# A six-layer graph network on one core: the first layer's second stretch with its gathered rows split into two f32r terms

## The reference

```python
xn = layernorm(x)
h = xn                                   # graph network, 6 layers
for layer in range(6):
    agg = segment_sum(h[src], dst)       # gather a row per edge, add it to its node
    z = relu(batchnorm((h + agg) @ W1[layer] + b1[layer]))
    z = batchnorm(z @ W2[layer] + b2[layer])
    h = z if layer == 5 else relu(z)
# mixing, 8 heads of 32 columns: k, v = layernorm of xn per head (two weight sets)
mix = q @ (k^T v / N) + xn
x = x + h + mix
y = layernorm(x)
x = x + sum_e softmax(y @ Wr + br)_e * expert_e(y)   # 8 experts, 3 matrices each
```

## Time and profile before

| What | Value |
|---|---|
| median of the runs | 4614.98 us (4611.78 to 4618.43) |
| profiled execution | 4616.16 us, its span 4614.4 us |
| mean granted TensorE clock | 0.981 |
| busy, of the span | PE 95%, PEld 70%, DVE 66%, ACT 68%, POOL 65% |
| fp32 matmuls of gathered quads (L975) | 1072, from 84.8 to 817.9 us |
| f32r matmuls of gathered quads (L978) | 1750, from 969.4 us on |

### The profile page before, as it was taken

How to read it: one execution, slowest core, us unless ns; L and a number is a source line. 1 busy time by engine, 2 the same in 40 slices (tenths; PEclk the granted TensorE clock), 3 DMA queues, 4 the chain that set the end, 5 groups by cost and what they waited for, 6 DMA issues and landing times.

```text
span 4614.4 us, 69574 instructions
## 1 busy us (share of the span) xinstructions
PE 4399.7 (95%) x18931; PEld 3237.0 (70%) x18931; DVE 3056.1 (66%) x7493; ACT 3122.7 (68%) x4292; POOL 2987.3 (65%) x3420
## 2 busy tenths in 40 slices
PE   4999899999999999999998999999998899999999
PEld 3666688578866888578875888668875766666665
DVE  6888766466665666656765666656665466666666
ACT  5767533488866888578876888578875555555555
POOL 5777766057771777447772777637773277778786
PEclk8999999999999999999999999999999799999999
DMA  6444644065543555255543555345554000000000
GB/s 228 159 136 154 214 155 145 17 201 177 172 137 123 179 177 172 80 178 181 171 146 115 176 180 162 115 142 187 172 157 170 10 3 6 8 9 8 9 8 9
DMA packets 198882, 571.18 MB, mean 124 GB/s; under 512 B 44498, under 2 KB 63420, under 8 KB 198396
## 3 DMA queue, kind: packets, MB, share of 16 engines
q0 software_dynamic: 109728, 299.78, 22.3%
q1 hardware_dynamic: 81404, 238.40, 14.8%
q10 hardware_dynamic: 7392, 28.90, 1.6%
HBM read 487.16 MB, written 79.74 MB: 123 GB/s over the span
## 4 chain that ended last, share of the span: by engine, by line
PE 75%; issue 6%; POOL 5%; DVE 5%; ACT 4%; DMA 3%; ACTq 0%; DVEq 0%; POOLq 0%; SPq 0%
PE bank L1077 33%; PE bank L1287 12%; PE bank L1296 7%; PE bank L978 6%; PE bank L1172 5%; PE bank L975 4%; POOL BIG L799 4%; PE bank L1021 3%; DMA BIG<-y_table,idx 2%; PE bank L1106 1%; ACT Z L1339 1%; ACT bank L1374 1%; PE bank L986 1%; DVE BIG L1628 1%; DMA G<-y_table,idx 1%
## 5 line engine op out<-in xcount | busy, mean ns | idle before, releaser
L799 POOL DMA_INDIRECT BIG<-y_table,idx x1750 | 1665.7, 952 | 575.4 <-issue 521.5
L1077 PE MATMUL bank<-Ac,Ych 128*128 128x512 f32 x6204 | 1474.8, 391 | 0.0
L1077 PEld LDWEIGHTS bank<-Ac,Ych 128*128 128x128 f32 x6204 | 1164.4, 188 | 244.4 <-issue 1.0
L1393 ACT CAST Ac<-BIG 128x2048 fp32r<-128x2048 uint8 (+1 forms) x426 | 738.7, 1748 | 183.7 <-PE bank L978 89.5
L1644 DVE TENSOR_TENSOR Gsp<-bank,Gsp 128x512 fp32r<-128x512 f32 x870 | 559.7, 683 | 226.6 <-ACT bank L1374 225.7
L1768 DVE TENSOR_TENSOR Z<-Z,bank 128x512 f32 x546 | 375.2, 687 | 462.6 <-PE bank L978 270.7
L799 POOL DMA_INDIRECT G<-y_table,idx x536 | 536.8, 1001 | 199.1 <-issue 154.8
L2140 DVE TENSOR_TENSOR G<-G,bank 128x448 f32<-128x448 f32 x784 | 461.4, 618 | 218.5 <-ACT G L1565 112.8
L1367 ACT CAST Gsp<-BIG 128x1024 fp32r<-128x1024 f32 (+1 forms) x455 | 461.1, 1014 | 165.2 <-DMA BIG<-y_table,idx 150.6
L1374 ACT COPY bank<-BIG 128x512 f32<-128x512 f32 x870 | 481.0, 583 | 127.3 <-DVE Gsp L1644 127.2
L1654 DVE TENSOR_SCALAR onehot<-iota,rel 128x128 fp32r<-128x128 f32 x2290 | 517.1, 302 | 11.2 <-PE bank L975 6.6
(11 more groups left out here) (233 smaller groups left out, 6104.9 us busy)
## 6 DMA issues: line engine op xcount, KB each, us to landing
BIG<-adjacency SPq DMA_DIRECT2D x273, 448.0 KB, 3.6
BIG<-y_table,idx POOLq DMA_INDIRECT x1750
BIG<-y_table SPq DMA_DIRECT2D x27, 896.0 KB, 5.8
y_table<-BIG SPq DMA_DIRECT2D x25, 896.0 KB, 3.9
adjacency<-BIG ACTq DMA_DIRECT2D x7, 3136.0 KB, 12.5
BIG<-in_x SPq DMA_DIRECT2D x14, 896.0 KB, 8.4
G<-y_table,idx POOLq DMA_INDIRECT x536
y_table<-BIG ACTq DMA_DIRECT2D x7, 896.0 KB, 3.6
```

The lines of the kernel that those rows point to most:

```text
L799: nc.gpsimd.indirect_dma_start(out=rows[:, j, :], out_offset=None, in_=y_table, in_offset=bass.IndirectOffsetOnAxis(ap=idx[:, t:t + 1], ax ...
L1077: last = mm(bank[2 * (k % 2) + b][:, 0:UW], Ych[pos % 2][:, i, s, b * P:(b + 1) * P], cast_place(l, x_)[:, i - CA * h, :], start=(i == 0 a ...
L1393: nc.scalar.copy(cast_place(l, x_)[:, 0:t1 - t0, :], Land[k % NL][:, t0:t1, :]).then_inc(s_ac, 1)
```

## The change

In steps n >= N1 of the first layer a quad is handled as in the later layers:

- *Buffers.* Three buffers `Gsp0`: two in `G` (over the old `raw0`), the third in `BIG` at the place of the third `Ac`, so two `Ac` are left for the first layer's casts (`casts` returns 2). The raw rows land in the low half of the buffer itself (`raw_split`), on new semaphores `s_gx`. `place0` gives the buffer, quad 91 the second one, quad 92 the first, quad 93 the third.
- *Gather.* Quad n waits for quad n - 3. Quad 91 waits for quad 90 and quad 92 for quad 89, the last ones in their place. Quad 93 waits for the store of the last adjacency block; ScalarE's cast no longer does.
- *ScalarE.* `quad_high(n)` behind the casts of step n: one copy 128x1024, rounded. The square root `mixing` comes behind it and a step later (`set_at(n, 2)`).
- *VectorE.* `quad_low(n)` at the head of step n: one in-place subtraction 128x1024. Groups of the second stretch are evicted by the 128x512 reduction.
- *TensorE.* `quad(n)` goes behind the dense halves and the transposes of step n, ahead of the mixing product; one 512 wide f32r matmul per tile.

```diff
         def casts(l):
-            return NAC if first_layer(l) else NACL
+            return NAC - 1 if first_layer(l) else NACL
+        def place0(n):
+            return (N1 % RQ0 // 2, 1 - N1 % RQ0 // 2, 2)[(n - N1) % 3]
+        def last_there(n):
+            if n >= N1 + 3:
+                return n - 3
+            return max((m for m in range(N1) if m % RQ0 // 2 == place0(n)), default=None)
...
             def gather(l, n):
                 rows, s_rows, _ = gathered(l, n)
-                if first_layer(l):
+                if first_layer(l) and n >= N1:
+                    if last_there(n) is not None:
+                        hold(pool, s_mmq, last_there(n) + 1)
+                    else:
+                        hold(pool, s_fl[(S - 1) % 2], (S - 1) // 2 * LANES + LANES)
+                elif first_layer(l):
...
-                    if first_layer(l):
+                    if not is_split(l, n):
                         last = mm(group_bank(g)[:, 0:D], onehot[:, q, j, :].bitcast(fp32), rows[:, j, :],
                                   start=start, stop=stop)
                     else:
                         last = mm(group_bank(g)[:, 0:2 * D], onehot[:, q, j, :],
-                                  Gsp[n % RQ][:, j, :, :].rearrange("p k f -> p (k f)"), start=start, stop=stop)
+                                  split_place(l, n)[:, j, :, :].rearrange("p k f -> p (k f)"), start=start, stop=stop)
...
                 for n in range(quads(l)):
-                    if first_layer(l):
+                    if first_layer(l) and n < N1:
                         quad(l, n)
...
                     if first_layer(l):
+                        if n >= N1:
+                            quad(l, n)
                         if set_at(n, MIX_LAG) is not None:
...
                 act.wait_ge(s_rows, there)
+                if first_layer(l):
+                    nc.scalar.copy(split_place(l, n)[:, 0:tiles(n), 0, :], rows[:, 0:tiles(n), :]).then_inc(s_gh, 1)
+                    return
...
-                if first_layer(l) and x_ == NAC - 1:
-                    act.wait_ge(s_fl[(S - 1) % 2], (S - 1) // 2 * LANES + LANES)
...
                             half(x_)
-                        if set_at(n, 1) is not None:
-                            mixing(set_at(n, 1))
+                        quad_high(l, n)
+                        if set_at(n, 2) is not None:
+                            mixing(set_at(n, 2))
...
             def quad_low(l, n):
-                dve.wait_ge(s_gh, (l - 1) * N1 + n + 1)
+                dve.wait_ge(s_gh, split_before(l) + n + 1)
+                if first_layer(l):
+                    there = split_place(l, n)
+                    tt(there[:, 0:tiles(n), 1, :], gathered(l, n)[0][:, 0:tiles(n), :],
+                       there[:, 0:tiles(n), 0, :].bitcast(fp32), ALU.subtract).then_inc(s_gl, 1)
+                    return
...
-                if first_layer(l):
+                if first_layer(l) and g < NGR:
                     V.tensor_copy(grow[:, g % 2, :], group_bank(g)[:, 0:D]).then_inc(s_ev, 1)
                 else:
                     V.tensor_reduce(grow[:, g % 2, :], group_bank(g)[:, 0:2 * D].rearrange("p (k f) -> p f k", k=2),
...
-                    elif not first_layer(l):
+                    else:
                         quad_low(l, n)
```

More of the change, by code:

```diff
@@ L197, in gps_layer @@
         raw = [at(QUAD_BYTES + q * RAW_BYTES, RAW_BYTES).rearrange("p (j f) -> p j f", j=GJ) for q in range(RQ)]
+        Gsp0 = Gsp[0:2] + [f32r_at("Gsp0x", [P, GJ, 2, D], BIG_AT + QUAD_BYTES + RQ * RAW_BYTES)]
+        low_half = lambda a: a.rearrange("p (j k f) -> p j k f", j=GJ, k=2)[:, :, 1, :]
+        raw_split = [low_half(G[:, q * QUAD_BYTES // 4:(q + 1) * QUAD_BYTES // 4]) for q in range(2)]
+        raw_split += [low_half(at(QUAD_BYTES + RQ * RAW_BYTES, QUAD_BYTES))]
+        assert AC_BYTES >= QUAD_BYTES
         raw0 = [G[:, q * GJ * D:(q + 1) * GJ * D].rearrange("p (j f) -> p j f", j=GJ) for q in range(RQ0)]
@@ L289, in gps_layer @@
         s_g0 = [sem(f"s_g0{q}") for q in range(RQ0)]
+        s_gx = [sem(f"s_gx{q}") for q in range(len(Gsp0))]
         s_g = [sem(f"s_g{q}") for q in range(RQ)]
@@ L426, in casts, with is_split, split_before, split_place @@
         def casts(l):
-            return NAC if first_layer(l) else NACL
+            return NAC - 1 if first_layer(l) else NACL
         def cast_place(l, x_):
             return Acx if x_ % casts(l) == NAC else Ac[x_ % casts(l)]
+        def is_split(l, n):
+            return not first_layer(l) or n >= N1
+        def split_before(l):
+            return -N1 if first_layer(l) else (l - 1) * N1 + N0 - N1
+        def place0(n):
[4 more added lines that the diff above has]
+            return max((m for m in range(N1) if m % RQ0 // 2 == place0(n)), default=None)
+        def split_place(l, n):
+            return Gsp0[place0(n)] if first_layer(l) else Gsp[n % RQ]
         def gathered(l, n):
+            if first_layer(l) and n >= N1:
+                q = place0(n)
+                return raw_split[q], s_gx[q], sum(tiles(m) for m in range(N1, n + 1) if place0(m) == q) * LANES
             if first_layer(l):
@@ L795, in gather @@
                 elif n >= RQ:
-                    hold(pool, s_gh, (l - 1) * N1 + n - RQ + 1)
+                    hold(pool, s_gh, split_before(l) + n - RQ + 1)
                 for j in range(tiles(n)):
@@ L967, in quad @@
                 rows, s_rows, there = gathered(l, n)
-                if first_layer(l):
+                if is_split(l, n):
+                    pe.wait_ge(s_gl, split_before(l) + n + 1)
+                else:
                     pe.wait_ge(s_rows, there)
-                else:
-                    pe.wait_ge(s_gl, (l - 1) * N1 + n + 1)
                 for j in range(tiles(n)):
                     start, stop = first and j == 0, last_ and j == tiles(n) - 1
-                    if first_layer(l):
+                    if not is_split(l, n):
                         last = mm(group_bank(g)[:, 0:D], onehot[:, q, j, :].bitcast(fp32), rows[:, j, :],
@@ L1371, in quad_high @@
                 if n > 0 or not (isinstance(l, int) and l == 1):
-                    act.wait_ge(s_gl, (l - 1) * N1 + n)
+                    act.wait_ge(s_gl, split_before(l) + n)
                 for j in range(0, tiles(n), 2):
```

## The result

The changed kernel takes 4631.06 us (median of 7 runs, 4620.81 to 4632.44), the kernel before 4616.06 (median of 7): ratio 1.0028, 95% interval 1.0018 to 1.0038. Predicted were 4610, range 4592 to 4628. It is slower by a little, where no change was the likeliest. The profiled execution took 4620.81 us (span 4619.1).

The account below looks back on a forecast made before the run. VectorE was to take over from TensorE as the bound: start 557 + work 257.5 + waits 5 + tail 3 = 822.5 us for the last group's add, against 826.94 before, so 4610 us in all, range 4592 to 4628.

Parts of the forecast that it names:

- TensorE's part: First layer's second stretch, from quad 94: one f32r matmul per tile instead of two fp32, 35.7 us less TensorE work.
- VectorE's sum: From step 94 to the last group's add: VectorE's work sums to 257.5 us for 45 steps, 5.7 a step.
- The start: Seam at quads 90 to 94: later gathers let VectorE start step 94 at 557 us, 2 us either way.
- Between: Steps from 94 on: VectorE's waits, 1.8 us in 18 steps, 5 us in 45, bounds 0 to 15.
- walk of eighteen steps: From 557 us, eighteen steps priced engine by engine: VectorE waited twice, 0.8 and 1.0 us.
- the walk's example: Step 102, two dense halves: cast delays the high term, ready at 611.6 us, wanted by VectorE at 610.9.
- The tail: Last three steps of the stretch: little for VectorE, a double half for TensorE, 3 us more.
- rival 2: Stretch bound by three gather buffers taking turns: some 20 us more, last add 842, total 4630; chance 0.16.
- Its sign: What would show rival 2: VectorE gaps before the low term, for the high term, at each double half.
- Rival 1: TensorE stays the stretch's bound: 35.7 us less, 9 lost to the later start, about 4588; chance 0.12.
- Rival 3: GpSimd bounds the stretch: each low term lengthens one gather, 42 us in all, about 4612; chance 0.06.
- the prediction's last warning: Forecast wrong if TensorE's gaps in the stretch grew enough for its clock to fall, as to 0.75 earlier.

Follow-up runs that it names:

- e1: Kernel before, unsplit, with quad 91's gather waiting for quad 90 and quad 93's for the last adjacency store; first W1 part at 837.66 us, 10.6 late.
- e11: Changed kernel with each quad's four gathers from quad 94 on replaced by one plain load; stretch 282.1 us, whole-time ratio 0.9992.
- e2: Kernel before, unsplit, with two cast buffers in the first layer instead of three; first W1 part at 829.37 us, 2.3 late.
- e4: Changed kernel with five filler matmuls on TensorE in the step behind each mixing half; stretch 279.3 us for 278.6.
- e5: Changed kernel with ScalarE's square root back one step earlier, ahead of the high term; stretch 303.8 us, whole-time ratio 1.0040.
- e6: Changed kernel with VectorE taking the next quad's low term ahead of the first mixing half; first W1 part at 857.28 us.
- e8: Changed kernel with ScalarE taking the high term ahead of the step's casts; first W1 part at 849.76 us.
- e9: Changed kernel with the two sums of the mixing statistics replaced by small copies on VectorE; first W1 part at 826.32 us.
- e13: Changed kernel with quads behind a mixing half left in fp32 (seven came out so); stretch 285.3 us.
- e15: Changed kernel with plain loads for the gathers and the high term ahead of the casts; stretch 273.7 us.
- e3: Changed kernel with the split beginning at quad 94, quads 91 to 93 left fp32; first W1 part at 836.75 us.
- e10: Changed kernel with split from quad 94, high term ahead of casts, next low term ahead of first mixing halves; first W1 part at 843.17 us.
- e14: Changed kernel with the split from quad 94 on and quads behind a mixing half left in fp32; stretch 289.6 us.

## Why the prediction was wrong

It put the last group's add at 822.5 us; it ended at 839.56. By its own terms:

- **TensorE's part**: right as work. The f32r quads take one matmul for a tile, and TensorE was not the bound.
- **VectorE's sum**: right, 257.5 predicted, 258.4 measured as what the waits leave of the stretch, the low term at 1.228 us alone.
- **The start**: 557 predicted, 561.10 measured, 4.1 us. Quad 91's gather came at 531.93 and quad 93's at 543.79, 0.9 us late each; what failed is the issue of quad 93, done at 552.2 instead of 547.9, because one of its gathers took 4.29 us. The next four stand behind it. The two added waits cost 10.6 us in the unsplit kernel (e1); the prediction had them in its sum as the date of the start, so only the 4.1 us are an error of it.
- **Between**: this is the step that failed, the term of the sum for VectorE's waits: 5 us predicted in 45 steps, 0 to 15 as its bounds, 16.7 measured. The mechanism was the one named (two cast buffers, the high term behind the cast, at steps with two dense halves), and all five waits of the same course lie there; the size was wrong. The prediction had TensorE idle some 25 us for VectorE (27.8 measured), but in its walk of eighteen steps this idling delayed nothing, and ScalarE was ahead by 0.3 to 7 us. In the trace the dense half behind a gap ends late, the cast waits for it, the high term for the cast, and VectorE pays its own delay back: 2.87 us at quad 103, where the walk's example had 0.7, and 4.01 and 4.70 at quads 115 and 134.
- **The tail**: 3 predicted, 3.3 measured.

4.1 + 0.9 + 11.7 + 0.3 = 17.0, the miss. That the measured 4631 is near rival 2's 4630 is luck on its side, as the next paragraph shows.

**The rivals.** Rival 2 had the number (842, 4630) and not the cause: it made the turn of three gather places the bound, and e11 takes issue and landing out of that turn without a shorter stretch. Its sign, gaps in front of the low term at each double half, was in part seen (at five of ten), and its remark that two cast buffers leave little play holds; the third buffer is worth 2.3 us in e2, unsplit. Rival 1 fell: TensorE idled. Rival 3 fell: GpSimd waited 36 us for TensorE in the stretch. But the gathers did lengthen: 167 of them, mean 1065 and 1086 ns, against the 0.95 of an undisturbed one, 20 us in all, where rival 3 had put 42. The one of 4.29 us ran from 546.62 to 550.91, and VectorE's two-input passes from 546.52 to 550.08, seven short ones and a low term without a break between them. It isn't chance: in the eight other kernels that split quads 91 to 93 (e4, e5, e6, e8, e9, e11, e13, e15) the same gather took 4.29 or 4.30 us; in e3, e10 and e14, which split from quad 94 on, no gather of the stretch took more than 2.0. The Trainium skill (SBUF — State Buffer, "SBUF: two separate sides") states that a VectorE instruction with two SBUF inputs and a GpSimd instruction that reads SBUF exclude one another for the whole instruction. These traces agree, and the mean shows that most gathers get through in between: the exclusion decided one date at the seam, not the pace. A lower clock in TensorE's gaps, the prediction's last warning, came true (0.73 in the ten us from 800). It is part of the largest waits (sixteen matmuls at 801.78 took 1.9 us longer than before), and e4 shows that filling the gaps gives nothing on balance.

**What is settled and what isn't.** Settled: quad 94 is 13.7 us late, and the two waits alone make 10.6 us of loss in the unsplit kernel. Behind it VectorE sets the pace: its 258 us of work, 50 of them new, and 20 us of waits fill the stretch, so that TensorE's 36 us don't come out. The waits are elastic: e9, e14 and e15 each took something away and saw part or all of it return as another wait. The late start is elastic too (e3), so the 13.7 us can't be added to a gain behind them. Not settled: how much of e5's and e13's length belongs to gaps that the program doesn't explain, and what a third cast buffer would be worth beside the split. As all five waits come where a cast buffer is needed again, that is the nearest rival to "the order is at fault", and it wasn't tried: the third split buffer takes the third cast buffer's place. No order was found that makes VectorE's waits vanish with gathers in place.

## What to carry to other kernels

When work moves from the full engine to one that is 65% busy, the new bound's sum of work is only a floor: add what it will wait, and look for that behind its own longest run of work. There the delay goes round through the other engines' queues and comes back to it, most of all where a buffer is needed again at once. A step moved forward helps only if its input is there; ask what stands behind it (e6, e8). Where two things can be late in front of one instruction, taking either away may show nothing; take both (e8, e11, e15).

## What the runs showed of the hardware

- One gather's issue took 4.29 us beside an unbroken run of two-input passes on VectorE, at the same place in nine kernels; in the kernel before the longest took 1.95.
- TensorE's granted clock was 0.50, the lower of its two levels, from 540 to 552 us, behind idle time from 531 to 546; its first four wide matmuls took 2.06 us where they take 1.17 at the upper level. The gaps inside the stretch cost 0.03 on the mean (0.97 from 575 to 840), and holding it at 1.00 with filler matmuls shortened nothing (279.3 us for 278.6).
